# Row maxima of the attention scores reduced in parts of one 512-key tile instead of groups of two, in an adaLN attention and mixture-of-experts kernel

## The reference

```python
mod = (silu(c) @ wmod).reshape(2, 6, 1, 256)
sa, ca, ga, sb, cb, gb = the six rows of mod
ga, gb = sign * maximum(abs, 0.25)
h = layernorm(x) * (1 + ca) + sa
q, k, v = (h @ W_q + b_q) @ W_s, h @ W_k + b_k, h @ W_v + b_v     # 16 heads of 16
attn = softmax(q @ k.T / 4) @ v                                   # 2 x 16 heads, 2048 x 2048
x = x + ga * (attn @ W_o + b_o)
h = layernorm(x) * (1 + cb) + sb
x = x + gb * moe(h)     # 8 experts, each takes its top 512 tokens, 256 -> 1024 -> 256
```

## Time and profile before

| | |
|---|---|
| median of 3 runs | 1737.43 us (1731.07, 1737.83, 1737.43) |
| profiled execution, span | 1734.7 us, no other time of it is recorded |
| PE busy | 1685.5 us (97%), 17251 instructions |
| DVE busy | 1513.5 us (87%), 1908 |
| ACT busy | 1291.7 us (74%), 2454 |
| POOL busy | 229.3 us (13%), 300 |
| line 230, group maxima | 1024 instructions, 1191.6 us |
| line 1080, exponentials | 2048 instructions, 1079.4 us |

### The profile page before, as it was taken

One profiled execution on the slowest core, in us unless ns is written; L12 is line 12 of the kernel. 1 busy time (PEld: TensorE's weight loads), 2 busy tenths in 40 slices (PEclk: granted clock), 3 DMA queues, 4 the chain that ended last, 5 costly groups with the idle time before them and its releaser, 6 DMA issues. The chain is left out here.

```text
span 1734.7 us, 43731 instructions
## 1 busy us (share of the span) xinstructions
PE 1685.5 (97%) x17251; PEld 969.8 (56%) x17251; DVE 1513.5 (87%) x1908; ACT 1291.7 (74%) x2454; POOL 229.3 (13%) x300
## 2 busy tenths in 40 slices
PE   8999999999999999999999999999999998599998
PEld 5645555555555555555555554555555586488887
DVE  5678999999999999999999999999999476687774
ACT  2327888888888888888888888888888834365663
POOL 0422012100010000001000000100000012135433
PEclk9999999999999999999999999999999997599999
DMA  8660443222222223323222223342220331235332
GB/s 265 207 178 24 92 98 53 41 41 39 52 55 39 41 49 52 47 40 65 41 42 39 39 41 54 59 60 39 41 42 12 108 107 61 98 101 143 89 82 37
DMA packets 93658, 122.03 MB, mean 70 GB/s; under 512 B 24060, under 2 KB 70716, under 8 KB 90348
## 3 DMA queue, kind: packets, MB, share of 16 engines
q1 hardware_dynamic: 84492, 109.22, 28.1%
q0 software_dynamic: 6144, 8.39, 2.7%
q10 hardware_dynamic: 2816, 1.61, 0.3%
HBM read 79.35 MB, written 38.54 MB: 68 GB/s over the span
## 5 line engine op out<-in xcount | busy, mean ns | idle before, releaser
L230 DVE TENSOR_REDUCE pmax<-ps 128x2 f32<-128x1024 f32 x1024 | 1191.6, 1215 | 54.2 <-PE ps L223 50.2
L1080 ACT ACTIVATE pt<-ps 128x512 f32<-128x512 f32 x2048 | 1079.4, 600 | 179.8 <-PE ps L584 157.7
L223 PE MATMUL ps<-kp,qp 48*128 48x512 f32 x2048 | 622.4, 458 | 2.9 <-DVE pmax L230 2.9
L1139 PE MATMUL ps<-pt,v_st 128*32 128x256 f32 (+1 forms) x10752 | 589.7, 334 | 0.7 <-ACT pt L1080 0.7
L584 PE MATMUL ps<-qp,kp 50*128 50x512 f32 x2048 | 560.8, 422 | 0.5 <-ACT pt L1080 0.5
L584 PEld LDWEIGHTS ps<-qp,kp 50*128 50x128 f32 x2048 | 292.5, 185 | 265.2 <-ACT pt L1080 263.1
L1139 PEld LDWEIGHTS ps<-pt,v_st 128*32 128x32 f32 x10752 | 265.7, 109 | 261.0 <-issue 187.2
L223 PEld LDWEIGHTS ps<-kp,qp 48*128 48x128 f32 x2048 | 245.6, 184 | 108.1 <-issue 89.8
L213 POOL CAST m_parts<-rowmax_t 128x32 fp32r<-128x32 f32 x64 | 13.5, 211 | 864.5 <-DVE rowmax_t L247 864.5
L1752 PE MATMUL ps<-w_l,hid_h 128*128 128x256 f32 x256 | 72.3, 283 | 0.0
L446 ACT ACTIVATE pt<-ps,xb 128x512 fp32r<-128x512 f32 x32 | 21.8, 687 | 64.7 <-PE ps L613 63.7
(11 more groups left out here) (229 smaller groups left out, 1297.6 us busy)
## 6 DMA issues: line engine op xcount, KB each, us to landing
kp<-k_parts SPq DMA_DIRECT2D x186, 128.0 KB, 4.5
v_all<-L_ffn_w SPq DMA_DIRECT2D x16, 1024.0 KB, 6.9
qp<-q_parts SPq DMA_DIRECT2D x186, 64.0 KB, 4.1
k_parts<-pt SPq DMA_DIRECT2D x16, 512.0 KB, 3.4
q_parts<-pt SPq DMA_DIRECT2D x16, 512.0 KB, 2.9
o_rows<-o_sb SPq DMA_DIRECT2D x64, 128.0 KB, 3.4
sums_c<-o_rows SPq DMA_DIRECT2D x512, 0.5 KB
m_rows<-m_parts SPq DMA_DIRECT2D x256, 2.0 KB
```

The lines of the kernel that those rows point to most:

```text
L223: last = nc.tensor.matmul(slot[:, half * CH:(half + 1) * CH], qp[rows, r, a * P:(a + 1) * P], kp[rows, r, c * CH:(c + 1) * CH], start=True ...
L230: v.reduce_max(pmax[:, u % 2, 2 * k:2 * k + 2], slot.rearrange("p (f t) -> p f t", f=2), AX.X).then_inc(groups_out, 1)
L1080: nc.scalar.activation(pt[:, s % PTS, half * CH:(half + 1) * CH], bank(n % SCORE_BANKS), ACT.Exp, scale=SCALE).then_inc(scores_out, 1)
L1139: last = mm(acc[32 * j:32 * (j + 1), first * QB:(first + many) * QB], v_st[:, h % NBUF, kt, :], probs[:, :, j * QB:(j + 1) * QB], start=kt ...
```

## The change

A group is split into its parts: a part is 128 queries of one row half by 512 keys, one matmul into one PSUM bank and one `reduce_max` of 128 x 512. The four banks 3 to 6 become four slots of one part each. Before part n, TensorE waits until part n-4 is reduced. A unit has 32 parts, three in each block of three chunks, in the order G S S G S G, and two in the short block (G S S G). Each part takes the row half opposite to that of the chunk that it is paired with in this order (`part_places`), so the parts of a unit come in another order than the groups did. Code for folding two parts into one reduction comes with it and is switched off: `FOLD_BLOCKS` is empty, so `FIRSTS` and `SECONDS` are empty and no line that depends on them runs. The 25 groups that lie in the projections stay groups. `pmax` is laid out by key chunk, and `join_maxima` reads it so.

Beside it, `gates` makes only the two rows that are used, 512 columns in bank 6, `mod_row` has two rows instead of four, the copy of line 450 is half as long, and one `tensor_scalar` of GpSimd on an unused row goes.

```diff
+GROUP_SLOTS = 4
+PARTS = 2 * KT
+FIRST_PART = 2 * EARLY_GROUPS
+ALL_PARTS = UNITS * PARTS
+BLOCK_ORDER = "GSSGSG"
+SHORT_ORDER = "GSSG"
+FOLD_BLOCKS = ()
...
+def order_of(b):
+    return SHORT_ORDER if b == DELAY else BLOCK_ORDER
+def part_places():
+    halves, folds, chunk = [], [], 0
+    for b in range(BLOCKS):
+        order, at = order_of(b), []
+        for letter in order:
+            at.append(chunk % 2 if letter == "S" else None)
+            chunk += letter == "S"
+        for i in range(0, len(order), 2):
+            for j, other in ((i, i + 1), (i + 1, i)):
+                if at[j] is None:
+                    at[j] = 1 - at[other]
+                    halves.append(at[j])
...
+def reduced_until(n):
+    return EARLY_GROUPS + (n - FIRST_PART) - folds_until(n)
...
-        mod_row = sb("mod_row", [P, NB, 4, D])
+        mod_row = sb("mod_row", [P, NB, 2, D])
...
-            v.tensor_reduce(rowmax[:, 0:QT].rearrange("p (f a) -> p f a", f=2),
-                            pmax[:, u % 2, :].rearrange("p (a c f) -> p f a c", c=NCH, f=2),
+            v.tensor_reduce(rowmax[:, 0:QT], pmax[:, u % 2, :].rearrange("p (c q) -> p q c", c=NCH),
                             AX.X, ALU.max).then_inc(rowmax_made, 1)
...
-                    nc.scalar.copy(mod_row[:, n].rearrange("p m d -> p (m d)"), bank(6, 2)).then_inc(gates_out, 1)
+                    nc.scalar.copy(mod_row[:, n].rearrange("p m d -> p (m d)"), bank(6)).then_inc(gates_out, 1)
...
-                for half in range(2):
-                    for k in range(KD):
-                        last = mm(bank(6 + half), silu_b[:, k, b, :],
-                                  wmod_sb[:, k, 2 * D + half * 512:2 * D + (half + 1) * 512],
-                                  start=k == 0, stop=k == KD - 1)
+                for k in range(KD):
+                    rows = wmod_sb[:, k, 2 * D:6 * D].rearrange("p (m d) -> p m d", d=D)
+                    last = mm(bank(6).rearrange("p (m d) -> p m d", d=D), silu_b[:, k, b, :], rows[:, 0:4:3, :],
+                              start=k == 0, stop=k == KD - 1)
...
-            def group_slot(n):
-                return bank(5 - 2 * (n % 2), 2)
+            def part_slot(n):
+                return bank(3 + (n - FIRST_PART) % GROUP_SLOTS)
...
-                link(g.tensor_scalar(mod_row[:, :, 2, :], mod_row[:, :, 2, :], 1.0, None, ALU.add))
...
-                for n in range(EARLY_GROUPS, STEPS):
-                    u, k = divmod(n, KT)
+                def reduce_part(n):
+                    u, half, a, c, _ = part(n)
+                    at = part_at(half, a, c)
+                    dve.wait_ge(groups_full, EARLY_GROUPS + n - FIRST_PART + 1)
+                    v.reduce_max(pmax[:, u % 2, at:at + 1], part_slot(n), AX.X).then_inc(groups_out, 1)
...
+                for n in range(FIRST_PART, ALL_PARTS):
+                    u, p = divmod(n, PARTS)
...
+                    if part(n)[4] != "first":
+                        reduce_part(n)
+                    if p == first_reduced and u > 1:
+                        join(u - 1)
...
+                join(UNITS - 1)
...
-                def next_group(n):
+                def next_part(n):
...
+                    last = n - GROUP_SLOTS
...
-                    pe.wait_ge(groups_out, n - 1)
-                    fill_group(pe, n, group_slot(n))
+                    elif n == FIRST_PART + 2:
+                        pe.wait_ge(groups_out, EARLY_GROUPS)
+                    elif last >= FIRST_PART:
+                        pe.wait_ge(groups_out, reduced_until(last + 1))
+                    rows, col = slice(HALF * half, HALF * half + KROWS), (f * (QT // 2) + a) * P
+                    keys = kp[rows, r, c * CH:(c + 1) * CH]
+                    mm(part_slot(n), qp[rows, r, col:col + P], keys, start=True, stop=True).then_inc(groups_full, 1)
...
+                    order = order_of(b) + ("GG" if block == 2 * DELAY else "")
+                    for letter in order:
+                        if letter == "S":
+                            scores(pe, *divmod(chunk, 2))
+                            chunk += 1
+                        elif at < ALL_PARTS:
+                            next_part(at)
+                            at += 1
```

More of the change, by code:

```diff
@@ L67, with part, folds_until @@
 ROUNDS = sum(DIGITS)
+def order_of(b):
[12 more added lines that the diff above has]
+                    halves.append(at[j])
+        if b in FOLD_BLOCKS:
+            folds.append(len(halves) - 1)
+    half_at = {(LEAD * 2 + j) % PARTS: half for j, half in enumerate(halves)}
+    firsts = [(LEAD * 2 + j) % PARTS for j in folds]
+    tiles = [(a, c) for a in range(QT // 2) for c in range(NCH)]
+    done = EARLY_GROUPS - KT
+    table = {}
+    for half in range(2):
+        mine = [p for p in range(PARTS) if half_at[p] == half]
+        for places, left in ((mine[:done], tiles[:done]), (mine[done:], tiles[done:])):
+            for p in firsts:
+                if p in places:
+                    a = max(a for a, c in left if (a, FOLD_CHUNK) in left and (a, FOLD_CHUNK + 1) in left)
+                    table[p] = (half, a, FOLD_CHUNK, "first")
+                    table[p + 2] = (half, a, FOLD_CHUNK + 1, "second")
+                    left = [(t, c) for t, c in left if t != a or c < FOLD_CHUNK]
+            places = [p for p in places if p not in table]
+            assert len(places) == len(left)
+            for p, (a, c) in zip(places, left):
+                table[p] = (half, a, c, "alone")
+    assert sorted(table) == list(range(PARTS)) and all(table[p][0] == half_at[p] for p in table)
+    return table
+PLACES = part_places()
+FIRSTS = sorted(p for p in PLACES if PLACES[p][3] == "first")
+SECONDS = [p + 2 for p in FIRSTS]
+def part(n):
+    u, p = divmod(n, PARTS)
+    half, a, c, kind = PLACES[p]
+    return u, half, a, c, kind if u >= FOLD_UNIT else "alone"
+def folds_until(n, which=FIRSTS):
+    u, p = divmod(n, PARTS)
+    if u < FOLD_UNIT:
+        return 0
+    return (u - FOLD_UNIT) * len(which) + sum(q < p for q in which)
+def reduced_until(n):
+    return EARLY_GROUPS + (n - FIRST_PART) - folds_until(n)
 GATHER_SPARE = 14
@@ L229, in reduce_group, with join_maxima @@
             dve.wait_ge(groups_full, n + 1)
-            v.reduce_max(pmax[:, u % 2, 2 * k:2 * k + 2], slot.rearrange("p (f t) -> p f t", f=2),
+            at = k % NCH * QT + k // NCH
+            v.reduce_max(pmax[:, u % 2, at:at + QT // 2 + 1:QT // 2], slot.rearrange("p (f t) -> p f t", f=2),
                          AX.X).then_inc(groups_out, 1)
[L232 to L238, removed]
+            if n == KT:
+                join_maxima(dve, v, 0, KT)
+        def join_maxima(dve, v, u, reduced):
+            dve.wait_ge(groups_out, reduced)
             if u > 0:
                 dve.wait_ge(rowmax_turned, u)
-            v.tensor_reduce(rowmax[:, 0:QT].rearrange("p (f a) -> p f a", f=2),
-                            pmax[:, u % 2, :].rearrange("p (a c f) -> p f a c", c=NCH, f=2),
+            v.tensor_reduce(rowmax[:, 0:QT], pmax[:, u % 2, :].rearrange("p (c q) -> p q c", c=NCH),
                             AX.X, ALU.max).then_inc(rowmax_made, 1)
@@ L1025, in _ @@
                     stage_v(h, h)
-                link = links["pool"] = Link(pool, link_pool_sem)
-                link.base = 3
+                link = links["pool"]
                 sign, size = (stage_b[:, j, 0:NB * D].rearrange("p (b d) -> p b d", b=NB) for j in range(2))
-                for m in (0, 3):
+                for m in range(2):
                     gates = mod_row[:, :, m, :]
@@ L1091, in invert, with join, clear_seconds @@
                     inverse(v, f).then_inc(inverse_made, 1)
-                for n in range(EARLY_GROUPS, STEPS):
-                    u, k = divmod(n, KT)
+                def reduce_part(n):
[3 more added lines that the diff above has]
+                    v.reduce_max(pmax[:, u % 2, at:at + 1], part_slot(n), AX.X).then_inc(groups_out, 1)
+                def join(u):
+                    join_maxima(dve, v, u, reduced_until((u + 1) * PARTS))
+                def clear_seconds(u):
+                    for p in SECONDS:
+                        half, a, c, _ = PLACES[p]
+                        at = part_at(half, a, c)
+                        v.memset(pmax[:, u % 2, at:at + 1], LOWEST)
+                clear_seconds(0)
+                first_reduced = next(p for p in range(PARTS) if p not in FIRSTS)
+                for n in range(FIRST_PART, ALL_PARTS):
+                    u, p = divmod(n, PARTS)
                     done = u - 3
-                    if k == AHEAD % KT and done >= 0 and done // HALVES % HG == HG - 1:
+                    if p == 2 * (AHEAD % KT) and done >= 0 and done // HALVES % HG == HG - 1:
                         invert(done)
-                    reduce_group(dve, v, n, group_slot(n))
+                    if part(n)[4] != "first":
+                        reduce_part(n)
```

(7 more changed lines are left out.)

25 lines of the change are left out of this document (17 added, 8 removed).

## The result

The changed kernel takes 1724.4 us (median of 4 runs, 1721.8 to 1724.4), the kernel before 1736.1 on the same occasion; the ratio is 0.9933 with a 95% interval from 0.9914 to 0.9953. The forecast was 1725, the range 1709 to 1746. Ratios, and the median of the variant with five merged pairs, use the fast executions alone: one of the kernel before (1780 us) and two of that variant (2070 and 7570 us) were in a slower state and are left out. The profiled execution of after has a span of 1719.7 us against 1734.7, 15.0 less; its own time is 1721.8, the lowest of the four.

What follows compares the result with a forecast made beforehand. TensorE was taken to bound the attention, and VectorE after the change. Reductions -6.7, early leave -1.5 and gates -3.9 made -12.1 us on 1734.7, 1722.6; with 2.7 around the span, forecast 1725 us, range 1709 to 1746.

Steps and rivals of the forecast that it cites:

- TensorE bounds the unit before, 37 slots to 32: Attention on TensorE: 64 matmuls per unit take 37 pair slots of 0.23 us; the new order needs 32, 18.5 us.
- VectorE's step, taken as 0.599 from rows of other instructions: Attention on VectorE: 512-column reductions start 0.599 us apart, so 32 and the join need 19.48 us per unit.
- The rule that spoke against the change: VectorE's reductions: latency exposed between instructions makes the 512-column step 0.658 us, 21.4 us a unit, some 107 us slower.
- VectorE isn't starved with four slots: Attention: four slots hold 2.4 us of VectorE's work against 1.67 us without a fresh part, 0.7 us in hand.
- -8.2 us for the attention: Attention: -6.7 us from VectorE's reductions, joins and start, and -1.5 us from the last part leaving TensorE earlier.
- the early leave of the last part: End of the attention: last part leaves TensorE up to three reductions before it is taken; -1.5 us (0 to -1.8).
- -3.9 us for the gates: Gates, two batch rows: each saves 1.72 us of matmul records and 0.23 us of TensorE idle time; bounds -4.4 to 0.
- (a): Rival, attention on TensorE: pairs fall apart, 37 slots and 19.6 us a unit return, only the gates' -3.9 remains: 1733; chance 0.17.
- (b): Rival, VectorE in the attention: the step is 0.609 us, +20 us, so 1745; chance 0.12.
- (d): Rival, VectorE in the attention: half-size reductions don't overlap, 0.681 us each, 22.2 us a unit: 1892; chance 0.03.
- (e): Rival, VectorE in the attention: the small reduction is cheaper than the subtraction, 0.591 us, -16 us: 1709; chance 0.08.
- (c): Rival, start of a block: VectorE still starves, losing 1.19 us per unit, 20.67 us a unit, +74: 1799; chance 0.10.

Runs made afterwards that it cites:

- five merged pairs: Changed kernel with five of a unit's sixteen pairs of neighbouring parts each reduced by one 128 x 1024 instruction: 1735.6 us, ratio 1.0002 to the kernel before.
- two merged pairs: Changed kernel with two pairs of neighbouring parts per unit each reduced by one 128 x 1024 instruction: 1727.8 us, ratio 0.9954 to the kernel before.

## Why the prediction was right

The profiled spans: 1734.7 to 1719.7 us, -15.0 against the -12.1 of the sum.

- *TensorE bounds the unit before, 37 slots to 32.* Shown: a shorter reduction before leaves the unit at 19.63 us, a shorter one after moves the unit to 18.64 us (18.5 forecast), and with the pairs broken it is 20.97.
- *VectorE's step, taken as 0.599 from rows of other instructions.* The mean step is 0.597 us, duration 0.682 (0.681 forecast as the far end, if nothing overlapped). With the join 19.47 us a unit, 19.48 forecast, and that so close a match is in part luck: 32 steps came out 0.06 us shorter, and the join 0.06 us longer (0.37 instead of 0.31). Half of the latter is its first reduction, which reads `pmax` by another stride and takes 203 instead of 175 ns.
- *The rule that spoke against the change.* By 120 cycles plus one per column the Trainium skill ("VectorE: DVE Perf Modes", "The TRN2 errata") gives 0.658 us for an operation of 512 columns out of PSUM. Taken as a step, as the prediction took it, the trace contradicts it: 1929 steps from part to part show 0.597. What the Trainium skill says in that section on latency between instructions, it says of SBUF, out of which these reductions don't read.
- *VectorE isn't starved with four slots.* Its wait for TensorE is 0.2 us in 1998 parts. It holds narrowly: three slots leak 0.5 us a unit, and longer holds leak 0.2 to 0.5 us. For ScalarE the prediction set 0.60 us, a duration, against three exponentials per 1.83 us, which would leave nearly nothing. Their step is 0.49 us, so the conclusion stands with more room than the sum gave it.
- *-8.2 us for the attention.* The profiles: from the first exponential, 131.0 to 128.3 us, to the last, 1396.6 to 1383.1 (starts), it is -10.8, of which 1.7 belong to the clock (below). That leaves -9.1 against -8.2, and the parts-only kernel's ratio gives -8.2. From the first single reduction to the end of the last it is 1218.9 us for the 1220.5 of the sum, so -8.3 instead of -6.7, and the early leave of the last part gave -0.8 instead of -1.5. The start-up was sized about right; VectorE runs through almost at once:

```profile
134.48 2.67 DVE L1169 TENSOR_REDUCE pmax<-ps 128x1 f32<-128x512 f32 x4
137.31 6.67 DVE L1169 TENSOR_REDUCE pmax<-ps 128x1 f32<-128x512 f32 x11 [0.16 <-PE ps L1222]
```

- *-3.9 us for the gates.* This term was mis-sized: -2.7 in the profile, -1.7 (0.3 to 3.3) in the timing of it alone. I had named the condition ("a store holds the next chunks") and not priced it. The first batch row gives its share (-2.1), the second keeps only -0.2 of it and loses the rest to ScalarE, whose queue has three roundings that wait for DMAs ahead of the copy.
- *What the sum didn't have: the clock.* -1.7 us at 130.8 us and about -1.5 after the attention are differences of granted clock between the two profiled executions. The value products of chunk 7, in before and in after:

```profile
130.84 3.68 PE L628 MATMUL ps<-xb,pt 128*128 128x256 f32 x8
...
135.11 1.99 PE L628 MATMUL ps<-xb,pt 128*128 128x256 f32 x8
```

```profile
128.11 1.99 PE L700 MATMUL ps<-xb,pt 128*128 128x256 f32 x8
...
130.71 1.99 PE L700 MATMUL ps<-xb,pt 128*128 128x256 f32 x8
```

Eight records take 3.68 us in before and 1.99 in after, and the other eight 1.99 in both. Windows of before around the two places (the third number from the right is the granted clock):

```profile
130.00:135.00 5.00, 4.82 (x14) 3.05 (x14) 2.39 (x4) 0.60 (x1) 4.66 (x5) 0.66 0.43 160
1397.00:1440.00 43.00, 41.83 (x260) 37.83 (x261) 38.59 (x141) 10.65 (x21) 4.71 (x2) 0.96 0.39 129
```

After has 1.00 in both of the matching windows. The clock was at its lower level (1.2 GHz) for part of these stretches; before the first one TensorE had been idle 1.3 us for a group's slot, but it was so in after too, where the clock didn't fall. The kernel before with the shorter reduction also lacks the first stretch (its span is 1728.1 us), and the changed kernel with two merged pairs has it, at 128.6 us. What follows the last exponential takes 334.8 to 339.1 us over the profiles of all kernels, in no order of the changes. So I count both as something that comes and goes, and not as a gain of the change; the medians of several runs (-11.7) lie nearer to the sum than the two profiles do. That the median came out within 1 us of the forecast, with the gates 1.2 us short and the reductions 1.6 us over in the profiles, is luck; the intervals of the runs are about 3 us wide to either side.

The rivals: (a) pairs do fall apart, as the block of 2.13 us shows, but under VectorE's time; (b), (d) and (e) fall with the step of 0.597; (c) falls at four slots, and at three it stands with 0.5 us a unit instead of 1.19.

## What to carry to other kernels

Count what each engine needs per round on its own, from start-to-start steps and not from durations: an engine that is 95% busy and waits 0.2 us at a time has more to spare than its busy share says. When a change frees one bound, the next engine's sum sets the gain, here 0.17 of a possible 1.1 us a unit, and a cut of one operand (448 of 512 columns) in both kernels tells in two runs which engine holds the pace. Work taken off an engine ahead of a wait on a third party (the gates' copy behind DMAs) is only worth what that wait leaves.

## What the runs showed of the hardware

- A reduction of 128 x 512 floats out of PSUM lasts 0.682 us and follows the one ahead after 0.597; of 128 x 1024, 1.214 and 1.133. 0.08 us lies under the next one, in both. Starvation shows first as a lost overlap: with three slots a unit was 0.5 us longer at 2.0 us of idle time in 800, and 299 of 1929 steps lasted 0.67 to 0.70 us.
- Two matmuls of 48 to 50 rows in opposite row halves that are neighbours in the queue cost one slot of 0.23 us (0.34 us for the first behind the products); with parts and chunks of a pair in one half, the kernel took 91 us more (1815.8 against 1724.4).
- The join's reduction of 32 maxima to 8 took 194 to 203 ns over the profiles where the four inputs of a maximum lie 8 apart, and 175 to 176 ns in the layout of before, where they lie 2 apart.
